# Linear attention from high and low parts: keys, values and queries in three products each, and the queries' bias on ACT

## The reference

```python
x = x + 0.5 * tanh(layernorm(x) @ W1 @ W2 @ W3 + b)
x = x + linear_attention(layernorm(x))
x = x + 0.5 * tanh(layernorm(x) @ W1 @ W2 @ W3 + b)
x = x + 0.5 * spectral(layernorm(x))
x = x + causal_softmax_attention(layernorm(x))
x = x + 0.5 * spectral(layernorm(x))

def linear_attention(x):
    q = x @ Wq + bq                                   # 16 heads of 8
    k, v = split((x @ Wd + bd) @ Wu + bu)
    q, k = elu(q) + 1.0, elu(k) + 1.0
    context = einsum('bthd,bthe->bhde', k, v)
    z = 1.0 / (einsum('bthd,bhd->bth', q, k.sum(axis=1)) + 1e-06)
    return (einsum('bthd,bhde->bthe', q, context) * z) @ Wo + bo
```

## Time and profile before

| | us |
|---|---|
| runs | 1324.59, 1324.78, 1326.14 (median 1324.78) |
| profiled execution | 1325.28, span 1323.5 |
| PE busy over the span | 1247.6 (94%) |
| DVE busy | 1025.3 (77%) |
| ACT busy | 934.0 (71%) |
| POOL busy | 589.4 (45%) |
| first keys and values of LIN start | 60.12 |
| last keys and values of LIN start | 171.03 |

### The profile page before, as it was taken

The page is one execution under the profiler, slowest core; times in us unless marked ns, Lnnn a source line. Parts: engine busy times, 40 slices in busy tenths (PEclk is TensorE's granted clock), DMA queues, the critical chain, the costliest instruction groups (busy, mean ns, idle before and its releaser), DMA issues.

```text
span 1323.5 us, 38816 instructions
## 1 busy us (share of the span) xinstructions
PE 1247.6 (94%) x11323; PEld 1067.1 (81%) x11331; DVE 1025.3 (77%) x4813; ACT 934.0 (71%) x3265; POOL 589.4 (45%) x913
## 2 busy tenths in 40 slices
PE   5799987899999999999999999999999999999997
PEld 4688866778888888888888888888888888888885
DVE  6977779877777777777777777777777777777774
ACT  4745357577777777777777777777777777777773
POOL 4812137534444444444444444444444444444442
PEclk9999989999999999999999999999999999999999
DMA  8000000000000000000000000000000000000000
GB/s 212 1 1 0 1 1 0 1 2 1 2 9 0 8 0 8 0 8 0 8 0 8 0 8 0 8 0 8 0 8 0 8 0 8 0 8 0 9 1 17
DMA packets 14301, 11.80 MB, mean 9 GB/s; under 512 B 709, under 2 KB 12522, under 8 KB 14058
## 3 DMA queue, kind: packets, MB, share of 16 engines
q1 hardware_dynamic: 14240, 11.19, 3.2%
q10 hardware_dynamic: 10, 0.00, 0.0%
HBM read 7.00 MB, written 4.19 MB: 8 GB/s over the span
## 4 chain that ended last, share of the span: by engine, by line
PE 57%; ACT 17%; issue 11%; DVE 10%; POOL 2%; DMA 1%; SPq 1%; ACTq 0%; DVEq 0%; POOLq 0%
PE ps L1048 9%; ACT pr L759 9%; PE ps L1079 9%; PE ps L1088 9%; PE ps L1062 6%; PE ps L1033 5%; ACT qk_hi L744 4%; PE ps L1035 3%; PE ps L1034 3%; DVE qk_lo L505 3%; DVE pT L534 2%; PE ps L962 2%; PE ps L920 1%; ACT pT L768 1%; PE ps L980 1%
## 5 line engine op out<-in xcount | busy, mean ns | idle before, releaser
L759 ACT ACTIVATE pr<-ps,neg_max 128x128 f32<-128x128 f32 (+1 forms) x1024 | 424.6, 430 | 165.2 <-DVE neg_max L519 165.2
L325 POOL TENSOR_TENSOR pr<-pr,rinv 128x256 f32<-128x256 f32 x256 | 156.9, 613 | 572.9 <-DVE rinv L527 572.9
L519 DVE CUSTOM_DVE_ANT_0 ps<-ps,mask 128x128 f32<-128x128 f32 (+1 forms) x1024 | 329.2, 389 | 8.0 <-issue 6.2
L327 POOL TENSOR_TENSOR pr<-pr,rinv 128x512 f32<-128x512 f32 x256 | 266.3, 1040 | 0.0
L505 DVE TENSOR_TENSOR qk_lo<-ps,qk_hi 128x512 fp32r<-128x512 f32 x256 | 176.9, 691 | 114.6 <-ACT qk_hi L744 114.1
L759 ACT ACTIVATION_READ_ACCUMULATOR pr<-ps,neg_max 128x1 f32 x1024 | 218.1, 213 | 0.0
L1062 PE MATMUL ps<-ident,pr 128*128 128x128 f32 x1536 | 209.9, 272 | 1.9 <-POOL pr L327 0.9
L534 DVE COPY pT<-ps 128x512 f32<-128x512 f32 x256 | 175.2, 685 | 29.8 <-PE ps L1062 26.0
L1062 PEld LDWEIGHTS ps<-ident,pr 128*128 128x128 f32 x1536 | 179.3, 140 | 20.4 <-issue 2.2
L1079 PE MATMUL ps<-pT,space 128*64 128x256 f32 (+1 forms) x2048 | 194.9, 332 | 0.7 <-ACT pT L768 0.5
L1033 PE MATMUL ps<-x_hi,wqk_hi 128*128 128x256 f32 x512 | 169.8, 332 | 18.2 <-DVE qk_lo L505 14.0
(11 more groups left out here) (168 smaller groups left out, 2356.7 us busy)
## 6 DMA issues: line engine op xcount, KB each, us to landing
out<-x_all SPq DMA_DIRECT2D x16, 256.0 KB, 2.3
x_all<-L_attn_x SPq DMA_DIRECT2D x1, 768.0 KB, 6.3
x_all<-L_attn_x SPq DMA_DIRECT2D x1, 512.0 KB, 3.9
space<-L_attn_Q SPq DMA_DIRECT2D x1, 512.0 KB, 15.4
space<-L_attn_K SPq DMA_DIRECT2D x1, 512.0 KB, 9.6
space<-L_attn_V SPq DMA_DIRECT2D x1, 512.0 KB, 11.6
space<-L_attn_W SPq DMA_DIRECT2D x1, 512.0 KB, 12.0
dft_s<-dft SPq DMA_DIRECT2D x1, 192.0 KB, 2.9
```

The lines of the kernel that those rows point to most:

```text
L327: nc.gpsimd.tensor_tensor(pr[:, buf, :, 1:3, :].rearrange("p h b k -> p h (b k)"), pr[:, buf, :, 1:3, :].rearrange("p h b k -> p h (b k)") ...
L519: last = nc.vector.tensor_tensor_reduce(o, o, mask[:, T - w:T], -1.0, -MASKED, ALU.add, ALU.min, neg_max[:, j, 2 * h + qt:2 * h + qt + 1])
L759: last = nc.scalar.activation(dst, ps[:, BANK_S + 2 * j + h, qt * P:qt * P + w], ACT.Exp, bias=neg_max[:, j, at:at + 1], scale=-1.0, accum ...
```

## The change

The normalised and transposed x of LIN is split into a high part (`xl_hi`, ACT's copy out of PSUM, now a cast to float32r) and a low part (`xl_lo`, a new DVE function `x_lin_low`); the weights of keys and values and of queries are split once at the start (`wkv_hi`, `wkv_lo`, `wq_hi`, `wq_lo`). Each float32 product becomes three float32r products. The queries' bias is no longer a product on PE: it is loaded as a column `bq_col` and ACT adds it in exp; a second ACT pass writes max(a, 0) into `rq`, and phi of the queries is min(exp, 1) + rq. In LIN three of the four tiles are normalised by ACT (`ACT_TILES`), one by DVE.

```diff
-        rows = sb("rows", [1, 6 * D])
-        BQ, FFN_B, FFT_B, BO_B, KV_B = 0, D, 2 * D, 3 * D, 4 * D
+        rows = sb("rows", [1, 5 * D])
+        FFN_B, FFT_B, BO_B, KV_B = 0, D, 2 * D, 3 * D
...
-        FFN_LOADS, SMALL_LOADS, BIAS_LOADS = 3, 8, 5
+        FFN_LOADS, SMALL_LOADS, BIAS_LOADS = 3, 9, 4
...
-        ACT_TILES = {FFN1: 2, LIN: 2, FFN2: 2, SPEC1: 2}
+        ACT_TILES = {FFN1: 2, LIN: 3, FFN2: 2, SPEC1: 2}
...
-                split(rows[:, 0:4 * D], 0, 4 * D)
+                split(rows[:, 0:3 * D], 0, 3 * D)
...
             def bias_of_keys_values():
 
+                dve.wait_ge(su_ev, 5)
+                nc.vector.tensor_tensor(wkv_lo[:], ps[:, 4, 0:2 * D], wkv_hi[:].bitcast(F32), ALU.subtract)
+                nc.vector.tensor_tensor(wq_lo[:], wq_s[:], wq_hi[:].bitcast(F32), ALU.subtract).then_inc(wlin_ready, 1)
...
-                nc.vector.scalar_tensor_tensor(out=phq[:, j, :], in0=eq[:], scalar=1.0, in1=ps[:, LIN_Q, :],
-                                               op0=ALU.min, op1=ALU.max).then_inc(phi_ready, 1)
+                nc.vector.scalar_tensor_tensor(out=phq[:, j, :], in0=eq[:], scalar=1.0, in1=rq[:],
+                                               op0=ALU.min, op1=ALU.add).then_inc(phi_ready, 1)
+
+            def x_lin_low(g, j):
+                dve.wait_ge(xT_ready, count(g + (G + 1)))
+                if isinstance(g, Count) or g >= 2:
+                    dve.wait_ge(q_done, count(g - 1))
+                    dve.wait_ge(kv_done, count(g - 1))
+                nc.vector.tensor_tensor(xl_lo[:, j, :], ps[:, 0, :], xl_hi[:, j, :].bitcast(F32), ALU.subtract).then_inc(xllo_ready, 1)
...
-                         [(3, g_norm(LIN)), (0, z_and_y), (5, g_stats(LIN)), (1, phi_k), (1, phi_q), (1, context_mask),
+                         [(3, g_norm(LIN)), (0, z_and_y), (5, g_stats(LIN)), (1, phi_k), (1, phi_q), (1, context_mask), (2, x_lin_low),
...
-                nc.scalar.activation(eq[:], ps[:, LIN_Q, :], ACT.Exp, bias=-1.0).then_inc(eq_ready, 1)
+                nc.scalar.activation(eq[:], ps[:, LIN_Q, :], ACT.Exp, bias=bq_col[:])
+                nc.scalar.activation(rq[:], ps[:, LIN_Q, :], ACT.Relu, bias=bq_col[:]).then_inc(eq_ready, 1)
...
-                pe.wait_ge(xT_ready, count(g + (G + 1)))
+                pe.wait_ge(xllo_ready, count(g + 1))
...
-                        last = mm(bank[:, t * 2 * D:(t + 1) * 2 * D], xT[:, j, (2 * k + t) * P:(2 * k + t + 1) * P],
-                                  wkv[:], start=False, stop=True, skip_group_check=True)
+                        at, o = slice((2 * k + t) * P, (2 * k + t + 1) * P), bank[:, t * 2 * D:(t + 1) * 2 * D]
+                        mm(o, xl_hi[:, j, at], wkv_hi[:], start=False, stop=False, skip_group_check=True)
+                        mm(o, xl_hi[:, j, at], wkv_lo[:], start=False, stop=False, skip_group_check=True)
+                        last = mm(o, xl_lo[:, j, at], wkv_hi[:], start=False, stop=True, skip_group_check=True)
...
-                if above_0(2 * g):
-                    pe.wait_ge(phi_ready, count(2 * g))
-                mm(ps[:, LIN_Q, :], bias_bf[:, BQ:BQ + D], ones_bf[:], start=True, stop=False, skip_group_check=True)
-                mm(ps[:, LIN_Q, :], wq_s[:], xT[:, j, :], start=False, stop=True, skip_group_check=True).then_inc(q_done, 1)
+                if above_0(g):
+                    pe.wait_ge(eq_ready, count(g))
+                o = ps[:, LIN_Q, :]
+                mm(o, wq_hi[:], xl_hi[:, j, :], start=True, stop=False, skip_group_check=True)
+                mm(o, wq_hi[:], xl_lo[:, j, :], start=False, stop=False, skip_group_check=True)
+                mm(o, wq_lo[:], xl_hi[:, j, :], start=False, stop=True, skip_group_check=True).then_inc(q_done, 1)
```

More of the change, by code:

```diff
@@ L141, in build @@
         w23 = sb("w23", [P, D]); wc = sb("wc", [P, D])
-        wkv = sb("wkv", [P, 2 * D])
+        wkv_hi = sb("wkv_hi", [P, 2 * D], F32R); wkv_lo = sb("wkv_lo", [P, 2 * D], F32R)
+        wq_hi = sb("wq_hi", [P, D], F32R); wq_lo = sb("wq_lo", [P, D], F32R); bq_col = sb("bq_col", [P, 1])
         abT = sb("abT", [P, 2, D]); circ = sb("circ", [P, D])
-        bias_bf = sb("bias_bf", [P, 6 * D], BF16)
+        bias_bf = sb("bias_bf", [P, 5 * D], BF16)
         kvrow = sb("kvrow", [1, 2 * D])
-        rest = sb("rest", [1, 2, 4 * D])
+        rest = sb("rest", [1, 2, 3 * D])
         wqk_hi = sb("wqk_hi", [P, 2, H * DQ], F32R); wqk_lo = sb("wqk_lo", [P, 2, H * DQ], F32R)
@@ L162, in build @@
         th = sb("th", [P, 2, GW])
-        eq = sb("eq", [P, GW]); ek = sb("ek", [P, GT, P])
+        xl_hi = sb("xl_hi", [P, 2, GW], F32R); xl_lo = sb("xl_lo", [P, 2, GW], F32R)
+        eq = sb("eq", [P, GW]); rq = sb("rq", [P, GW]); ek = sb("ek", [P, GT, P])
         phq = sb("phq", [P, 2, GW]); phk = sb("phk", [P, GT, P])
@@ L191, in build @@
         shift_ready = sem("shift_ready"); neg_mean_ready = sem("neg_mean_ready")
-        xn_ready = sem("xn_ready"); xn_act_ready = sem("xn_act_ready"); tr_done = sem("tr_done"); xT_ready = sem("xT_ready")
+        xn_ready = sem("xn_ready"); xn_act_ready = sem("xn_act_ready"); tr_done = sem("tr_done"); xT_ready = sem("xT_ready"); xllo_ready = sem("xllo_ready"); wlin_ready = sem("wlin_ready")
         mm_done = sem("mm_done"); th_ready = sem("th_ready"); x_ready = sem("x_ready")
@@ L383, in bias_parts @@
                 dve.wait_ge(in_bias, 16 * BIAS_LOADS)
-                nc.vector.tensor_scalar(rows[:, BQ:BQ + D], rows[:, BQ:BQ + D], 1.0, None, ALU.add)
                 rowstep(nc.vector.tensor_scalar(rows[:, FFT_B:FFT_B + D], rows[:, FFT_B:FFT_B + D], 0.5, None, ALU.mult))
-                split(rows[:, 0:4 * D], 0, 4 * D)
+                split(rows[:, 0:3 * D], 0, 3 * D)
                 nc.vector.memset(kvrow[:, 0:1], 0.0).then_inc(bias_ready, 1)
             def bias_of_keys_values():
+                dve.wait_ge(su_ev, 5)
+                nc.vector.tensor_tensor(wkv_lo[:], ps[:, 4, 0:2 * D], wkv_hi[:].bitcast(F32), ALU.subtract)
+                nc.vector.tensor_tensor(wq_lo[:], wq_s[:], wq_hi[:].bitcast(F32), ALU.subtract).then_inc(wlin_ready, 1)
                 dve.wait_ge(su_pe, 5)
@@ L632, in _ @@
         def _(act):
-            for done, dst, src in ((in_bias, rows[:, FFN_B:FFN_B + D], ffn_bias.unsqueeze(0)), (in_bias, rows[:, BQ:BQ + D], bq.unsqueeze(0)),
+            for done, dst, src in ((in_bias, rows[:, FFN_B:FFN_B + D], ffn_bias.unsqueeze(0)), (in_small, bq_col[:], bq.unsqueeze(1)),
                                    (in_bias, rows[:, FFT_B:FFT_B + D], fft_bias.unsqueeze(0)),
@@ L650, in small_out @@
                 act.wait_ge(su_pe, 5)
-                nc.scalar.copy(wkv[:], ps[:, 4, 0:2 * D])
+                nc.scalar.copy(wkv_hi[:], ps[:, 4, 0:2 * D])
+                nc.scalar.copy(wq_hi[:], wq_s[:])
                 nc.scalar.mul(circ[:], ps[:, 2, D:2 * D], 0.5 / D).then_inc(su_ev, 1)
@@ L693, in f @@
                             act.wait_ge(mm_done, count(g + (phase * G - 1)))
-                    nc.scalar.copy(xT[:, j, :], ps[:, 0 if phase == LIN else j, :]).then_inc(xT_ready, 1)
+                    if phase == LIN:
+                        nc.scalar.copy(xl_hi[:, j, :], ps[:, 0, :]).then_inc(xT_ready, 1)
+                    else:
+                        nc.scalar.copy(xT[:, j, :], ps[:, j, :]).then_inc(xT_ready, 1)
                 return f
@@ L911, in f @@
                     pe.wait_ge(xn_act_ready, count(n + 1))
-                    if phase == LIN or isinstance(g, int) and g == 0:
+                    if phase == LIN and above_0(g):
+                        pe.wait_ge(xllo_ready, count(g))
+                    elif phase == FFN2 and isinstance(g, int) and g == 0:
+                        pe.wait_ge(xllo_ready, G)
+                    elif phase == LIN or isinstance(g, int) and g == 0:
                         if above_0(n):
@@ L955, in keys_values @@
                     pe.wait_ge(su_ev, 5)
+                    pe.wait_ge(wlin_ready, 1)
                     pe.wait_ge(bias_ready, 2)
```

## The result

The changed kernel takes 1345.74 us (median of 5 runs, 1343.54 to 1348.07; before 1324.78). The ratio is 1.0152, 95% interval 1.0137 to 1.0168: slower by some 21 us. The profiled execution took 1346.56, span 1344.8. I had forecast 1323.8, and 1327.6 as the upper end: the forecast was wrong, by an effect that it does not name.

The account below looks back on a forecast made before the run. PE and a ring through ACT, DVE and PE were taken as balanced at 7.37 us a turn. Gaining 3.5 over thirteen turns, paying 2.05 at the entry and 0.5 at the end, took 1324.78 to 1323.8; range 1320.0 to 1327.6.

Parts of the forecast that it names:

- Keys and values, queries, phi of the keys: PE's turn: keys and values 1.84 us (0.32 less), queries 0.69 (0.38 less), idle 0.3 to 0.5 before the context.
- Only the 0.32 lies on it: Linear-attention turn: only the 0.32 us saved on keys and values shortens the PE–ACT–DVE cycle, 7.37 to 7.05; queries' 0.38 becomes waiting.
- The second ring: Linear-attention turn through ACT's two passes over the queries, DVE's phi and mask, then PE's numerators, keys and values: 7.15 us.
- 0.06 to PE: Linear-attention turn: the step from the end of DVE's mask to PE's numerators, taken as 0.06 us.
- the 0.05 that I allowed for PE's restart: Linear-attention turn: PE's restart after waiting for the mask, 0.05 us more at the upper end, priced by no row.
- the sign that I had named for a wrong forecast: Profile after: the mask, not phi of the keys, holding PE for more than 0.2 us a turn.
- the second pass sets the turn: Rival: ACT's two column-bias passes take 0.80 us each, the turn stays 7.37, no gain is left: 1327.3; chance 0.05.
- The entry: Start of the linear-attention stage: first keys and values 2.05 us later (weights 0.55, third tiles 0.78, low part 0.72); bounds 1.4, 2.3.
- The clock: Rival at the stage's entry: PE's pause grows to 2.67 us and halves its clock, +3.8 (or +1.8), 1327.6; chance 0.25.
- The end: Last turns of the linear-attention stage, where DVE is the chain: 0.5 us lost in all, bounds 0 and 0.8.

Follow-up runs that it names:

- the placed kernel: Changed kernel with the head of ACT's softmax loop put at slot 0 of a fetch block, nothing else different: 1327.94 us.
- the transposes: Against the placed kernel: twelve transposes of the identity, which nothing reads, added on PE ahead of the first keys and values; 1325.73 us.

## Why the prediction was wrong

**The step that failed** is the first sentence on what the change reaches: "The change touches only the linear-attention stage and the few microseconds at its two ends". I counted what each new instruction takes and what it waits for, and not that it moves the code behind it. ACT's softmax loop lies 23 instructions later, ACT then waits at each of 13 jumps back, and that costs 17.8 of the 21 us. The kernel with 23 idle copies and the kernel with its loop placed show it from both sides. No term of the sum and no rival stood for it, and the upper end of the range could not hold it.

Without that loss, as the placed kernel has it, the time is 1327.94, where I forecast 1323.8. That part goes by the sum's own terms:

- **Keys and values, queries, phi of the keys: right.** 1.87 for 1.84; queries 0.78 (116.63 to 117.41) for 0.69; PE waits 0.41 for phi of the keys, where I said 0.3 to 0.5. "Only the 0.32 lies on it" is right: with the mask out of the way a turn is 7.07, for 7.05 forecast.
- **The second ring: mis-sized.** I made it 7.15; it is 7.35. ACT's second pass is 0.71 for 0.69, so its price was right. The step "0.06 to PE" was wrong: that is what passes from phi of the keys to the context (122.91 to 122.97), and it still does so after the change. Behind the mask the sequencer's work for two more waits follows in the loop, which nobody saw as long as PE came later than the mask. Now weight load and numerators start 0.22 and 0.25 behind it; the 0.05 that I allowed for PE's restart, at the upper end alone, should have been 0.19. (The numerators take 1.05 for 0.98, and phi of the queries, which lets the mask start after 0.61 in place of 0.68, gives that back.) From context to numerators PE needs 2.30 (118.42 to 120.72) in place of 2.10: the mask holds it for 0.20, at the edge of the sign that I had named for a wrong forecast. From the second to the fourteenth keys and values the change gains 88.17 - 87.29 = 0.9 us in twelve turns, where I had 3.2; with the bias on PE it is 3.7. So the rival "the second pass sets the turn" came true, but by the restart behind the mask and not by passes of 0.80, and its chance of 0.05 was too low.
- **The entry: near in sum, by luck in part.** The start moved by 1.99 for 2.05 in the profiled run of the change. But 0.43 of it is the third load of x, which DVE had at 23.16, before at 22.73. The weights and bias rows behind it add 0.47 (DVE's next statistics at 29.43, before at 28.53) for 0.55, and the third tiles and the low part the remaining 1.09 for 1.50. The prediction let DVE's wait for x cover the bias column and gave a later x no price. In the placed kernel, whose entry is the same code, the start is 3.0 later (63.11) and x comes at 23.63, so one execution is not the last word.
- **The clock: the rival came true.** The granted clock read 0.50 from 62 to nearly 68, and the first turn took 8.52 for 7.10 before. I gave it 0.25 for want of more than one such pause; its price, 1.8 to 3.8, was above the 1.4 to 1.5 us of the first turn, and the time fell by 2.2 with the transposes. Over all 13 profiled executions the clock fell at the entry in the seven with a pause of 2.25 and in none of the six with 0.89 to 1.56. The Trainium skill's rule (TensorE: Matmul & The Clock Gate, Part 1), that the throttled state is the default and activity releases it, fits that. At the stage's end, after pauses of 2.42 to 2.50, the clock fell in ten executions and stayed at 1.00 in three (the bias on PE, the placed kernel with transposes, slot 208): such a pause can cost the clock, and does not always.
- **The end: smaller.** The last two steps between keys and values take 7.95 and 7.69, before 8.08 and 7.56: no change in sum. From there to the last transposes of y it takes 0.1 more. I had 0.5 for both.

So in the profiled run: entry 1.99, first turn 1.42, twelve turns -0.88, end 0.1, together 2.6 of the 2.65 seen. The remainder is a loss where I forecast a gain because of two terms: 2.3 us of the turns' gain held back by the mask, and 1.4 of the clock.

## What to carry to other kernels

Instructions have a place as well as a duration. Where a loop may outgrow what an engine holds, count the instructions that a change puts ahead of it, look for waits on "issue" at the first instruction behind a jump back and at the instruction queue's packets, and put the loop's head at a fixed slot, so that edits elsewhere cannot move it.

A wait that was free because its engine came late can cost once the engine comes early: here PE started 0.25 behind the mask where I had counted 0.06. So when two rings are within some tenths of each other, price the second one with the restart, and put the wait that comes last at the end of the list. And when a ring through other engines bounds the turn, ask on which engine a piece of work is hidden: the bias as a product of 0.22 us on PE cost the turn nothing, as a pass of 0.71 us on ACT it cost 0.28 a turn.

## What the runs showed of the hardware

- A jump back of ACT's loop took 0.3 us to the next instruction in the kernel before and 2.6 us in the changed one, where the code is loaded again; 65 packets more of the instruction queue (0.53 MB) are 5 packets, some 41 KB, for each of 13 jumps.
- The same loop of 302 instructions waits at no jump back with its head at slot 208 of a block, and at 13 with its head at slot 224.
- In loop turns PE's weight load follows the mask by 0.22 when the wait for it stands ahead of the other waits' register work, and by 0.12 and 0.06 in turn when it stands behind it.
- After a pause of PE of 2.25 us the granted clock fell to 0.50 in seven of seven profiled executions; after one of 0.89 to 1.56 us at the same place in none of six; after 2.42 to 2.50 us at the stage's end in ten of thirteen.
